# Preparation pipelined by blocks of rows and unrolled; weights of 12 heads combined from raw fp32 in the first chunk's slots; high parts in a slot's first unit

## The chip, the cores and the metric

The kernel runs on one core of a Trainium2 chip. The metric is the device time of one execution in microseconds. TensorE (PE) multiplies, VectorE (DVE), ScalarE (ACT) and GpSimd (POOL) work elementwise, and SyncE (SP) and ScalarE issue the transfers (DMA) between HBM and the on-chip memory.

## The reference

The input is x (2048 rows of 512). It is normalised (xn), and the result is x + attention(xn) + ffn(xn).

```python
q = (x @ wq.T).reshape(B, S, N_HEADS, QK_HEAD)          # 16 heads, 128 + 64
q_nope, q_pe = (q[..., :NOPE], q[..., NOPE:])
q_pe = apply_rope(q_pe, cos, sin)
kv = x @ wkv_a.T                                        # 128 latent + 64 rotary
k_pe = apply_rope(k_pe[:, :, None, :], cos, sin)[:, :, 0, :]
q_lat = jnp.einsum('bshd,hdc->bshc', q_nope, wkv_b_h[:, :NOPE])
kv_cache = rmsnorm(kv_lat, kv_norm_w)
scores = (einsum('bshc,btc->bsht', q_lat, kv_cache) + einsum('bshr,btr->bsht', q_pe, k_pe)) * SCALE
attn = jax.nn.softmax(where(causal, scores, NEG_INF), axis=-1)
out_lat = jnp.einsum('bsht,btc->bshc', attn, kv_cache)
out = jnp.einsum('bshc,hdc->bshd', out_lat, wkv_b_h[:, NOPE:])
attention = out.reshape(B, S, N_HEADS * VDIM) @ wo.T
# ffn: weight rounded to -1, 0, 1 times its mean absolute value, then xn @ w.T + bias
```

## The kernel before

A value of fp32 is held as a sum of two parts of the type fp32r, a high and a low one (names in _h and _l; in Wq, Wp, Wv and xT an index 0 or 1), and a product is made of three: high by high, high by low, low by high. ScalarE mostly writes the high part and VectorE or GpSimd the low one.

Two stages follow each other. `build_prepare` is the preparation. Its loop runs over 4 rounds (the first and last written out, two in a loop on each engine); a round holds one chunk of 512 rows as 4 blocks of 128, and the weights of 4 heads, spread over 16 places s. Places 0 to 3 transpose the normalised blocks (xhat to xT, L774, L550, L647), places 4, 5, 7, 9 make the latent rows and the rotary keys (pKV, L781; GpSimd's powers L471), places 8 to 11 the ffn (pF with ffnT, L800; acc, L655), places 12 to 15 transpose the keys (L812, L814). A head's weights take four places: wo is transposed (L824), the rotary part of wq is put in order by a product with a 0/1 matrix (L833), Wq is the product of wq and wkv_b (pQ, L843) and Wv that of wkv_b and wo (L849). GpSimd writes the low parts of the raw weights (L444, L449, L453). All weights, xT and acc of three chunks go to scratch tensors in HBM. No engine has a queue of its own beside the written order.

`build_attention` is the second stage. It runs over 64 heads of chunks (4 chunks of 16 heads), in slots: a slot of the first chunk is one head and has 4 units; in unit u row block u of the head is scored. In a slot s TensorE makes the scores of head s (p_score, L1124), the latent query of head s+1 (p_lat, units 1 and 2, L1104), in odd slots the rotary queries of two heads (p_rot, unit 0), p_out of head s-2 (units 2 and 3, L1144) and p_result of head s-3 (L1156). The scores are copied to probs (ring of 3, L1196), ScalarE takes exp (L1301), VectorE turns 32x32 squares (L1218), and 16 transfers exchange the quarters (12 by SyncE, L1004, 4 by ScalarE, L1311). Then ScalarE writes the high part of the exchanged probabilities (pT_h, L1322, `high_group`), and GpSimd the low one (pT, L1416). `high_place` says in which slot and unit that stands. A SyncE slot issues the first 8 transfers of an exchange, then the next head's Wv (L1016), which waits for the last p_result product of the head before, then the last 4 of the exchange.

```python
    if k < HIGH_RING:
        return (s + 1, units_of(s + 1) - 1) if phase(s + 1) == 1 else (s + 2, 0 if phase(s + 1) == 3 else 1)
```

## Time and profile before

| what | value |
|---|---|
| median of 3 runs (lowest, highest) | 1833.46 us (1831.61, 1834.55) |
| profiled execution: its time, its span | 1835.66 us, 1833.6 us |
| busy PE, DVE, POOL, ACT | 1715.1, 1210.3, 1008.5, 848.9 us |
| preparation ends, first p_rot product | 175.89 us |
| first score product of slot 0 | 184.8 us |
| DMA in all | 309.12 MB, mean 169 GB/s |

Busy time is the union of an engine's instructions. A matmul's record reaches until its result is out, so neighbours overlap, and the distance of two starts says more of what one costs than its length. PEclk is the granted TensorE clock, 1.00 for 2.4 GHz and 0.50 for 1.2 GHz.

### The profile page before, as it was taken

The numbers are of one execution on the slowest core, as the hardware profiler recorded it, in microseconds if no ns is written. First come the engines' busy times: TensorE is split into PE (matmuls) and PEld (weight loads), VectorE is DVE, ScalarE is ACT, GpSimd is POOL, SyncE is SP. The second block draws the span as 40 slices with busy tenths as digits, with TensorE's granted clock in tenths as the row PEclk, the third lists the DMA queues.
The fourth block names the chain that finished last, engine by engine and source line by source line (L and its number), as shares of the span: only waits on it lengthen the run. The fifth ranks groups of instructions, "written<-read, shape, count | busy, mean of one in ns | idle before, by whom it ended". The sixth has DMA issues, their size and how long they took to land. (4 is left out here: it accounts for less than half of the span.)

```text
span 1833.6 us, 28210 instructions
## 1 busy us (share of the span) xinstructions
PE 1715.1 (94%) x9326; PEld 1448.6 (79%) x9326; DVE 1210.3 (66%) x2801; ACT 848.9 (46%) x1358; POOL 1008.5 (55%) x635
## 2 busy tenths in 40 slices
PE   6998788888999999999999999999999999999996
PEld 5887677666777777778888888888888888888885
DVE  4765465665677667667777767767677666666763
ACT  4554344443444455345544554544544544554442
POOL 4674544443465555455565565565646555565654
PEclk9888899998999999999999999999999999999999
DMA  6995345464766666647555555566756565555553
GB/s 198 372 331 212 105 138 172 134 203 135 196 164 169 173 164 170 195 133 207 151 155 161 144 153 159 158 191 164 191 131 152 146 163 130 158 153 129 148 131 107
DMA packets 127680, 309.12 MB, mean 169 GB/s; under 512 B 29554, under 2 KB 42099, under 8 KB 126388
## 3 DMA queue, kind: packets, MB, share of 16 engines
q1 hardware_dynamic: 98784, 227.04, 44.0%
q10 hardware_dynamic: 28756, 80.35, 16.1%
q8 instruction: 72, 1.18, 0.3%
q14 instruction: 68, 0.56, 0.1%
HBM read 113.28 MB, written 34.60 MB: 81 GB/s over the span
## 5 line engine op out<-in xcount | busy, mean ns | idle before, releaser
L1416 POOL TENSOR_TENSOR pT<-pT,pT_h 128x1024 fp32r<-128x1024 f32 x320 | 688.8, 2181 | 419.8 <-ACT pT_h L1322 418.2
L1196 DVE TENSOR_SCALAR_CACHE_REDUCE probs<-p_score 128x512 f32<-128x512 f32 (+3 forms) x640 | 381.4, 602 | 370.4 <-PE p_score L1124 219.3
L1301 ACT ACTIVATE probs<-probs,neg_max 128x128 f32<-128x128 f32 (+15 forms) x256 | 307.6, 1202 | 438.0 <-DVE neg_max L1202 373.8
L1322 ACT ACTIVATE pT_h<-pT 128x1024 fp32r<-128x1024 f32 x320 | 291.3, 963 | 254.7 <-PE p_out L1144 173.6
L1218 DVE STREAM_TRANSPOSE turned<-probs 128x1024 f32<-128x1024 f32 (+7 forms) x384 | 341.6, 915 | 42.5 <-ACT probs L1301 38.0
L1144 PE MATMUL p_out<-pT_h,V_h 128*128 128x256 f32 (+3 forms) x1024 | 302.7, 296 | 26.6 <-POOL pT L1416 26.5
L1144 PE MATMUL p_out<-pT,V_h 128*128 128x256 f32 (+3 forms) x1024 | 304.2, 297 | 0.0
L1144 PE MATMUL p_out<-pT_h,V_l 128*128 128x256 f32 (+3 forms) x1024 | 303.7, 297 | 0.0
L1124 PE MATMUL p_score<-Kp,qp_h 128*128 128x512 f32 (+3 forms) x640 | 236.3, 369 | 15.3 <-POOL qp_l L1408 15.3
L1124 PE MATMUL p_score<-Kn_h,q_h 128*128 128x512 f32 (+3 forms) x640 | 241.6, 377 | 2.9 <-DVE q_l L1241 2.4
L1144 PEld LDWEIGHTS p_out<-pT_h,V_h 128*128 128x128 f32 x1024 | 196.8, 192 | 51.4 <-issue 34.8
L1124 PE MATMUL p_score<-Kn_l,q_h 128*128 128x512 f32 (+3 forms) x640 | 235.3, 368 | 0.0
L1124 PE MATMUL p_score<-Kn_h,q_l 128*128 128x512 f32 (+3 forms) x640 | 234.0, 366 | 0.0
L1124 PE MATMUL p_score<-Kp,qp_l 128*128 128x512 f32 (+3 forms) x640 | 233.1, 364 | 0.0
L1104 PE MATMUL p_lat<-xT,Wq 128*128 128x512 f32 x768 | 223.5, 407 | 0.0
L1259 DVE SCALAR_TENSOR_TENSOR acc<-p_result,inv_sum,acc 128x512 f32<-128x512 f32 x256 | 189.1, 744 | 42.6 <-PE p_result L1156 38.7
L1144 PEld LDWEIGHTS p_out<-pT_h,V_l 128*128 128x128 f32 x1024 | 197.1, 192 | 14.4
L1156 PE MATMUL p_result<-Wv,o_h 128*128 128x512 f32 x512 | 172.5, 418 | 31.3 <-issue 14.6
L1144 PEld LDWEIGHTS p_out<-pT,V_h 128*128 128x128 f32 x1024 | 197.1, 192 | 4.3
L1104 PEld LDWEIGHTS p_lat<-xT,Wq 128*128 128x128 f32 x768 | 140.6, 193 | 24.5
L1405 POOL TENSOR_TENSOR qp_l<-rotated,qp_h 64x512 fp32r<-64x512 f32 x64 | 82.3, 1286 | 140.7 <-ACT qp_h L1352 133.7
L1124 PEld LDWEIGHTS p_score<-Kp,qp_h 128*128 128x128 f32 x640 | 121.8, 190 | 40.1 <-POOL qp_l L1408 20.9
(135 smaller groups left out, 2352.0 us busy)
## 6 DMA issues: line engine op xcount, KB each, us to landing
pT<-turned SPq DMA_DIRECT2D x384, 128.0 KB, 3.3
Wq<-wq_scr ACTq DMA_DIRECT2D x63, 512.0 KB, 4.7
Wv<-wv_scr SPq DMA_DIRECT2D x63, 512.0 KB, 4.0
pT<-turned SPq DMA_DIRECT2D x192, 112.0 KB, 3.8
pT<-turned SPq DMA_DIRECT2D x192, 96.0 KB, 2.5
pT<-turned ACTq DMA_DIRECT2D x128, 128.0 KB, 3.9
Wp<-wp_scr SPq DMA_DIRECT2D x31, 512.0 KB, 4.7
pT<-turned SPq DMA_DIRECT2D x192, 80.0 KB, 2.8
```

The source lines that it names most:

```text
L1104: mm = pe.matmul(out, weights[:, w, it, :], xT[:, x, it, :], start=(it == 0 and k == 0), stop=(it == IT - 1 and k == 2))
L1124: mm = pe.matmul(out[:, 0:width], q[p][:, rows], kk[:, keys], start=(k == 0), stop=(k == 4 and b < j))
L1144: mm = pe.matmul(out[:, :, cols, :], v[:, t, :], pt[:, :, t - first, rest, :], start=(t == 0 and a == 0), stop=(t == piece_tiles(s) - 1 an ...
L1156: mm = pe.matmul(out[:, :], o[:, rows], Wv[:, w, :], start=(k == 0), stop=(k == 2))
L1196: dve.tensor_scalar(probs[row % ROW_RING][:, b * CW:b * CW + width], p_score[n % SCORE_RING][:, 0:width], SCALE, LOWEST, ALU.mult, ALU.max ...
L1218: last = dve.transpose(to.rearrange("p a t q -> p t a q"), rows.rearrange("p (t a q) -> p t a q", a=4, q=32))
L1259: dve.scalar_tensor_tensor(out=acc[:, i, :], in0=p_result[(QB * g + i) % 2][:, :], scalar=inv_sum[g % 4][:, i:i + 1], in1=acc[:, i, :], op ...
L1301: act.activation(probs[row % ROW_RING][:, 0:width], probs[row % ROW_RING][:, 0:width], ACT.Exp, bias=neg_max[p][:, i:i + 1], scale=1.0, ac ...
L1322: act.activation(high.rearrange("p r t i q -> p r t (i q)"), low.bitcast(F32).rearrange("p r t i q -> p r t (i q)"), ACT.Copy).then_inc(p_ ...
L1405: pool.tensor_tensor(qp_l[p][0:ROPE, :], rotated[own, :], qp_h[p][own, :].bitcast(F32), ALU.subtract).then_inc(qp_ready, 1)
L1416: pool.tensor_tensor(low.rearrange("p r t i q -> p r t (i q)"), low.bitcast(F32).rearrange("p r t i q -> p r t (i q)"), high.bitcast(F32). ...
```

## The change

The preparation's loop is replaced by 20 steps that are written out. Step n handles block n's transposes, block n-1's latent row, block n-2's ffn and block n-3's keys. Buffers that were one chunk wide (x_in, xT, acc, Wp) are there twice, and xhat is normalised by ScalarE with a shift and a scale. The host lays the weights out beforehand: transposed, the rotary rows in order, and per head one tensor `raw` of 128 x 1280 with wq, wo and both halves of wkv_b. Only heads 0 to 3 have Wq and Wv made in the preparation (8 products at steps 1 to 4 and 12 to 15). Those of heads 4 to 15 are made in slots 0 to 11 of the first chunk, in one fp32 product each instead of three of fp32r; raw weights lie in the unused upper columns of probs, staged results in the unused half of pT, and both go to scratch and are read back like before. Last, `high_place` puts the first three high parts of the first chunk's slots (two are there) in unit 0 instead of unit 1.

```diff
-LINEAR_SLOTS = {5: (0,), 6: (1,), 7: (2, 3)}
@@ high_place
-        return (s + 1, units_of(s + 1) - 1) if phase(s + 1) == 1 else (s + 2, 0 if phase(s + 1) == 3 else 1)
+        return (s + 1, units_of(s + 1) - 1) if phase(s + 1) == 1 else (s + 2, 0 if phase(s + 1) in (0, 3) else 1)
+RAW = 2 * D + 2 * RANK
+EARLY = 4
+LATE = H - EARLY
+BLOCKS = NT
+PREP_STEPS = BLOCKS + 4
+WEIGHT_STEPS = {1: 0, 2: 1, 3: 2, 4: 3, 12: 4, 13: 5, 14: 6, 15: 7}
+def raw_of(keep, g):
+    return keep["probs"][g % ROW_RING][:, CW:CW + RAW]
@@ build_prepare, tensor
+            def weights(w):
+                g = w // 2
+                pe.wait_ge(s_raw[g % ROW_RING], 16 * (g // ROW_RING + 1))
+                need(pe, s_w_l, w)
+                if w % 2 == 0:
+                    for it in range(IT):
+                        mm = pe.matmul(pQ[:, it, :], raw_query(keep, g, it), raw_keys(keep, g), start=True, stop=True)
+                else:
+                    mm = pe.matmul(pW[:, :], raw_values(keep, g), raw_output(keep, g), start=True, stop=True)
+                mm.then_inc(s_w, 1)
...
+            for n in range(PREP_STEPS):
+                if n < BLOCKS:
+                    transpose_x(n)
+                if 0 <= n - 1 < BLOCKS:
+                    latent(n - 1)
+                if 0 <= n - 2 < BLOCKS:
+                    linear(n - 2)
+                if 0 <= n - 3 < BLOCKS:
+                    transpose_keys(n - 3)
+                if n in WEIGHT_STEPS:
+                    weights(WEIGHT_STEPS[n])
@@ build_prepare, gpsimd
+            for n in range(PREP_STEPS):
+                if n < BLOCKS:
+                    add_bias(n)
+                if 0 <= n - 2 < BLOCKS:
+                    low_keys(n - 2)
+                if 0 <= n - 1 < BLOCKS:
+                    rotary_key(n - 1)
+                if n % QB == 2 and n // QB + 1 < NCH:
+                    norm(n // QB + 1)
+                if n % 2 and n // 2 < PAIRS:
+                    low_pair(n // 2)
@@ build_attention, sync
+            def load_weights(s):
+
+                sp.wait_ge(wq_made, s + 1)
+                sp.wait_ge(wv_made, s + 1)
+                load_raw(sp, t, keep, stored, s + EARLY + ROW_RING)
...
+                if 1 <= s <= LATE and s - 1 + EARLY + ROW_RING < H:
+                    load_weights(s - 1)
                 if 1 <= s <= SLOTS:
                     exchange(s - 1, (0, 1))
+                if 1 <= s <= LATE:
+                    store_query_weights(s - 1)
@@ build_attention, tensor
+            def make_query_weights(s):
+
+                g = s + EARLY
+                pe.wait_ge(stored["raw"][g % ROW_RING], 16 * (g // ROW_RING + 1))
+                pe.wait_ge(rot_read, (s + 1) // 2 + 1)
+                need(pe, wq_low, s)
+                out = p_rot[:, :].rearrange("p (a c) -> p a c", a=IT)
+                for it in range(IT):
+                    mm = pe.matmul(out[:, it, :], raw_query(keep, g, it), raw_keys(keep, g), start=True, stop=True)
+                mm.then_inc(wq_made, 1)
+
+            def make_value_weights(s):
+
+                g = s + EARLY
+                pe.wait_ge(q_split, s + 2)
+                pe.matmul(p_lat[:, :], raw_values(keep, g), raw_output(keep, g), start=True, stop=True).then_inc(wv_made, 1)
...
+                    if s < LATE and u == made_query_unit(s):
+                        make_query_weights(s)
+                    if s < LATE and u == QB - 1:
+                        make_value_weights(s)
@@ build_attention, scalar
+            def high_value_weights(s):
+                act.wait_ge(wv_made, s + 1)
+                need(act, wv_kept[s % 2], 16 * (s // 2))
+                act.activation(Wv_stage[s % 2][:, 0, :], p_lat[:, :], ACT.Copy).then_inc(wv_high, 1)
```

A piece of ScalarE's order in an even slot in the middle of the first chunk, before. The row ahead is exp of the previous slot's last row; L1311 is its share of the exchange, L1322 the high parts, L1345 the latent query's high part.

```order
L1301 ACTIVATE probs,row_sum<-probs,neg_max 128x512
L1328 ACTIVATE o_h<-p_out 128x4x4x32
L1301 ACTIVATE probs,row_sum<-probs,neg_max 128x128
L1311 DMA pT<-turned 32x512 x4
L1322 ACTIVATE pT_h<-pT 128x1024
L1322 ACTIVATE pT_h<-pT 128x8x64
L1301 ACTIVATE probs,row_sum<-probs,neg_max 128x256
L1301 ACTIVATE probs,row_sum<-probs,neg_max 128x384
L1345 ACTIVATE q_h<-p_lat 128x512
```

The same piece of the changed kernel, where L1262 is exp, L1272 the exchange, L1283 the high parts, L1318 and L1313 the new high parts of Wv and Wq (staged in pT).

```order
L1318 ACTIVATE pT<-p_lat 128x512
L1262 ACTIVATE probs,row_sum<-probs,neg_max 128x512
L1289 ACTIVATE o_h<-p_out 128x4x4x32
L1313 ACTIVATE pT<-p_rot 128x512
L1283 ACTIVATE pT_h<-pT 128x1024
L1283 ACTIVATE pT_h<-pT 128x8x64
L1262 ACTIVATE probs,row_sum<-probs,neg_max 128x128
L1272 DMA pT<-turned 32x512 x4
L1262 ACTIVATE probs,row_sum<-probs,neg_max 128x256
```

The high parts stand ahead of exp of row 0 (128x128) and of the exchange now, and the new high part of Wv ahead of exp of row 3 (128x512).

TensorE at the end of an odd slot of the changed kernel, unit 3: the last p_out products (L1085), then the two new products, then the scores of the next slot (L1065).

```order
L1085 MATMUL p_out<-pT_h,V_h 128x4x32
L1085 MATMUL p_out<-pT_h,V_l 128x4x32
L1085 MATMUL p_out<-pT,V_h 128x4x32
L1034 MATMUL p_rot<-probs 128x128 x4
L1041 MATMUL p_lat<-probs 128x512
L1065 MATMUL p_score<-Kn_h,q_h 128x128
L1065 MATMUL p_score<-Kn_l,q_h 128x128
```

The rows L1034 and L1041 are new; before, the scores followed p_out. In even slots L1034 stands at the end of unit 1.

TensorE in one step of the changed preparation (no weights in it), transposes first.

```order
L714 MATMUL pX<-ident,xhat 128x128 x4
L726 MATMUL pKV<-kvaT_h,xT_even 128x192
L726 MATMUL pKV<-kvaT_l,xT_even 128x192
L726 MATMUL pKV<-kvaT_h,xT_even 128x192 x2
L726 MATMUL pKV<-kvaT_l,xT_even 128x192
L726 MATMUL pKV<-kvaT_h,xT_even 128x192 x2
L726 MATMUL pKV<-kvaT_l,xT_even 128x192
L726 MATMUL pKV<-kvaT_h,xT_even 128x192 x2
L726 MATMUL pKV<-kvaT_l,xT_even 128x192
L726 MATMUL pKV<-kvaT_h,xT_even 128x192
L737 MATMUL pF<-ffnT,xT 128x512 x8
L744 MATMUL pK<-ident,lat 128x128
```

Before, the same kinds stood in four separate quarters of a round, between the weights' products.

## Rows read from the trace of the kernel before

**Rows 1.** The page, its first line.

```profile
span 1833.6 us, 28210 instructions
```

**Rows 2.** Stretches: us, busy us by engine, granted clock, DMA share, GB/s.

```profile
0.00:20.70 20.70, 3.94 (x12) 2.42 (x13) 6.20 (x18) 6.39 (x13) 4.55 (x9) 1.00 0.93 280
...
98.00:136.00 38.00, 35.61 (x216) 31.47 (x216) 25.50 (x58) 20.99 (x58) 26.91 (x39) 0.87 0.96 335
...
267.70:391.10 123.40, 109.73 (x528) 87.32 (x528) 78.73 (x204) 50.09 (x113) 54.48 (x37) 0.94 0.54 154
298.90:302.30 3.40, 3.40 (x9) 2.92 (x10) 1.70 (x3) 1.34 (x3) 2.93 (x3) 0.50 0.48 154
302.30:329.60 27.30, 24.06 (x124) 18.88 (x123) 17.99 (x48) 10.99 (x26) 10.45 (x7) 1.00 0.55 155
```

**Rows 3.** Order of time on PE, third round: start, us, line, out<-in.

```profile
113.77 0.63 PE L833 MATMUL pW<-order,wqp_h 64*128 64x64 f32 x4
...
114.78 0.33 PE L843 MATMUL pW<-wkb_h,wqn_h 128*128 128x128 f32 x1
...
116.17 0.30 PE L781 MATMUL pKV<-kvaT_h,xT 128*128 128x192 f32 x1
...
117.54 0.41 PE L849 MATMUL pW<-woT_h,wkb_h 128*128 128x512 f32 x1
...
118.26 2.02 PE L800 MATMUL pF<-ffnT,xT 128*128 128x512 f32 x8
120.11 0.60 PE L824 MATMUL pW<-ident,wo 128*128 128x128 f32 x4
120.47 0.34 PE L781 MATMUL pKV<-kvaT_h,xT 128*128 128x192 f32 x1
```

**Rows 4.** Groups on POOL in the preparation: count, busy us, mean ns.

```profile
L449 POOL TENSOR_TENSOR wqp_l<-wqp,wqp_h 64x512 fp32r<-64x512 f32 x16 | 22.3, 1395 | 2.3
...
L453 POOL TENSOR_TENSOR wqn_l<-wqn,wqn_h 128x512 fp32r<-128x512 f32 x16 | 20.4, 1277 | 2.6 <-POOL wqp_l L449 0.5
L444 POOL TENSOR_TENSOR wkb_l<-wkb,wkb_h 128x256 fp32r<-128x256 f32 x16 | 12.3, 767 | 25.6 <-ACT wkb_h L521 25.6
```

**Rows 5.** Order of time, the start and the end of the preparation.

```profile
9.26 2.04 PE L855 MATMUL pKV<-rows,ones 1*128 1x512 f32 x2 [9.26 <-DMA mask_f<-in_mask]
...
11.10 0.63 PE L856 MATMUL pKV<-rows,ones 1*128 1x128 f32 x2
...
12.56 2.46 DVE L625 BATCH_NORM_STATS2 stats<-x_in 128x6 f32<-128x512 f32 x4
...
18.96 1.03 POOL L459 TENSOR_TENSOR rstd<-var_eps,minus_half 128x4 f32<-128x4 f32 x1
...
20.72 1.09 PE L774 MATMUL pX<-ident,xhat 128*128 128x128 f32 x4 [7.52 <-DVE xhat L641]
...
26.63 0.42 PE L843 MATMUL pW<-wkb_l,wqn_h 128*128 128x128 f32 x1
...
26.84 0.41 PE L843 MATMUL pW<-wkb_h,wqn_l 128*128 128x128 f32 x1
...
175.89 1.52 PE L1104 MATMUL p_rot<-xT,Wp 128*128 128x512 f32 x3 [2.28 <-PEq L230]
```

**Rows 6.** First chunk: waits in 267.7:391.1 (us, times, longest), then order of time.

```profile
PE p_out L1144 <- POOL pT L1416: 7.2, 8, 1.5
...
PE p_result L1156 <- issue: 4.0, 4, 1.2
...
298.52 0.57 ACT L1345 ACTIVATE q_h<-p_lat 128x512 fp32r<-128x512 f32 x1
298.85 0.75 PE L1144 MATMUL p_out<-pT_h,V_h 128*128 128x512 f32 x1 [1.48 <-POOL pT L1416]
...
309.63 1.58 ACT L1322 ACTIVATE pT_h<-pT 128x1024 fp32r<-128x1024 f32 x2 [3.46 <-DMA pT<-turned]
...
329.46 0.57 ACT L1345 ACTIVATE q_h<-p_lat 128x512 fp32r<-128x512 f32 x1
```

More of the change, by code:

```diff
@@ L775, in transpose_x, with latent @@
                 mm.then_inc(s_xT, 1)
-            def product(out, b, w_h, w_l, done):
-                cols = slice(b * P, (b + 1) * P)
+            def latent(m):
+                cols, x = slice(m % QB * P, (m % QB + 1) * P), xT[m // QB % 2]
+                pe.wait_ge(s_xT_l, m + 1)
+                if m == 0:
+                    pe.wait_ge(s_bcast_out, 2)
+                    pe.wait_ge(s_kva_l, 2)
+                need(pe, s_lat, m - 1)
                 for it in range(IT):
-                    for k, (x, w) in enumerate(((0, w_h), (0, w_l), (1, w_h))):
-                        mm = pe.matmul(out, xT[:, x, it, cols], w[:, it, :], start=(it == 0 and k == 0),
+                    for k, (h, w) in enumerate(((0, kvaT_h), (0, kvaT_l), (1, kvaT_h))):
+                        mm = pe.matmul(pKV[m % 2][:, 0:192], x[:, h, it, cols], w[:, it, :], start=(it == 0 and k == 0),
@@ L798, in linear @@
+            def linear(m):
+                cols, x = slice(m % QB * P, (m % QB + 1) * P), xT[m // QB % 2]
+                if m == 0:
+                    pe.wait_ge(s_tern, 2)
+                need(pe, s_acc, m - 1)
                 for it in range(IT):
-                    for x in range(2):
-                        mm = pe.matmul(pF[b % 2][:, :], xT[:, x, it, cols], ffnT[:, it, :], start=(it == 0 and x == 0),
-                                       stop=(it == IT - 1 and x == 1))
+                    for h in range(2):
+                        mm = pe.matmul(pF[m % 2][:, :], x[:, h, it, cols], ffnT[:, it, :], start=(it == 0 and h == 0),
+                                       stop=(it == IT - 1 and h == 1))
@@ L934, in build_attention @@
         inv_sum = [sb(f"inv_sum{i}", [P, QB]) for i in range(4)]
+        spare = [half[:, :].rearrange("p (a k c) -> p a k c", a=4, k=2)[:, :, 1, :] for half in pT]
+        Wq_stage = [part[:, 0:2, :] for part in spare]
+        Wv_stage = [part[:, 2:4, :] for part in spare]
         p_score = [ps(f"p_score{i}") for i in range(SCORE_RING)]
@@ L1495, in constants, with laid_out @@
         "sinT": by_chunk(np.concatenate([sin, -sin, sin, -sin], 1)),
+    }
+def laid_out(wq, wkv_a, wkv_b, wo, w_ffn):
+    by_input = lambda w: np.ascontiguousarray(w.T.reshape(IT, P, -1).transpose(1, 0, 2))
+    apart = np.concatenate([np.arange(0, ROPE, 2), np.arange(1, ROPE, 2)])
+    heads = wq.reshape(H, QK, D)
+    pairs = heads[:, NOPE + apart, :].reshape(PAIRS, P, D)
+    keys_values = wkv_b.reshape(H, 2, P, RANK).transpose(0, 2, 1, 3).reshape(H, P, 2 * RANK)
+    return {
+        "raw": np.concatenate([heads[:, 0:NOPE, :], wo.T.reshape(H, VDIM, D), keys_values], axis=2),
+        "kvaT": by_input(wkv_a[np.concatenate([np.arange(RANK), RANK + apart])]),
+        "ffnT": by_input(w_ffn),
+        "wpT": np.stack([by_input(w) for w in pairs]),
     }
```

863 lines of the change are left out of this document (386 added, 477 removed).

## The prediction

> **What bounds the kernel now.** I read the busy row first, then the stretches, then the order of time inside two stretches. The profiled span is 1833.6 us [rows 1], its run 1835.66 us, the runs' median 1833.46 us. The change touches the preparation, which ends where the first p_rot product starts at 175.89 us [rows 5], and the first chunk (heads 0 to 15), whose heads 6 to 13 lie in 267.7:391.1 [rows 2]. What follows keeps its instructions and their order; I take its time as it is.
>
> In the preparation, one round (4 blocks of rows and 4 heads' weights) is 38.0 us long, and TensorE is busy 35.61 us of it while GpSimd is busy 26.91 and VectorE 25.50 [rows 2]. Busy overstates TensorE, because matmuls overlap. The starts in [rows 3] say what it needs at the full clock: 1.37 us for a block's 12 pKV products (116.17 to 117.54), 1.85 for its 8 pF products, 0.36 for 4 transposes (120.11 to 120.47), so with half of that again for the keys 1.37 + 1.85 + 0.36 + 0.18 = 3.8 us a block. A head's weights need 1.01 (8 order products), 1.39 (12 pQ products), 0.72 (3 wide ones) and 0.36 (wo transposes), 3.5 us. A round is 4 x (3.8 + 3.5) = 29.2 us, and takes 38.0: a factor of 1.30, made of waits between engines and of a granted clock of 0.87 [rows 2]. DMA is at a share of 0.96 there with 335 GB/s [rows 2], so it is full too, but each round is equally long whatever the traffic, so I hold the chain of TensorE for the bound.
>
> In the first chunk a pair of heads takes 30.94 us (q_h at 298.52 and 329.46 [rows 6]), 15.4 us a head. TensorE's columns per head are: p_lat 12 x 512, p_rot 6 x 512, scores 5 x 1280 and 4 masks of 128, p_out 3 x 1280, p_result 12 x 512, together 26,112. At 512 columns in 0.23 us (pF: 1.85 / 8) that is 11.7 us, with the narrow ones 12.0. So 3.4 us a head is not work. Of it 0.9 is the wait for the low part of pT (7.2 us over 8 heads), 0.5 a wait in front of p_result (4.0 us over 8), which I read as the Wv load, and half of 3.4 us at a granted clock of 0.50 in each pair, 0.85 a head [rows 2, 6]. That half-rate stretch begins right behind the 1.48 us gap at 298.85, and 302.3:329.6 is at 1.00.
>
> **The change, part by part.** (1) The preparation loses 12 heads' weights, and for the 4 left the order products, the wo transposes and the splitting into high and low parts. It becomes 20 steps, in each of which TensorE does one block's transposes, the pKV of the block before, the pF of the one before that, and keys. No round starts with only transposes any more.
>
> Start: the first TensorE transposes stand at 20.72 us, 8.2 us after x_in's statistics started at 12.56 [rows 5]. Now x and ffnT are issued first, 2.1 MB, at the 280 GB/s of the first 20.7 us [rows 2] 7.5 us, so statistics start near 8.3; 2.46 for them, 1.1 for moments, 1.03 for rstd [rows 5] put the first transposes near 14. The first pF products wait for VectorE: two copies, thresholds, comparison, kvaT_l and ternary, some 7 us more. I put step 2's start at 22 us, with TensorE then at half rate: matmuls at 26.63 and 26.84 are 0.21 apart where those at full rate are 1.39 / 12 = 0.12 apart [rows 3, 5].
>
> Steps 2 to 15: TensorE 3.8 us. GpSimd: 26.91 us a round less four times the three low parts it loses (1.395 + 1.277 + 0.767 = 3.44 [rows 4]) is 13.2, 3.3 a block, plus half a pair's low part, 0.64: 3.9 us. The two are level, so I take 4.4 us a step for hand-overs: 14 x 4.4 = 61.6. Seven weight products more: the fp32 ones are bounded by L855 and L856 [rows 5]. The first takes 1.84 us for 512 columns (9.26 to 11.10) at half rate, 0.92 at full; a 128-column one is between a quarter of it, 0.23, and half of L856's 0.63, 0.32. I take 0.28, so pQ's four cost 1.1 and the wide one 0.92: 7.1 us. Last four steps without new rows: 3.6 + 2.2 and the keys' chain, 8 us. Half rate at the start: 5 us. Sum 22 + 61.6 + 7.1 + 8 + 5 = 103.7, taken as 105: 71 us less. Bounds: 92 without any hand-over (22 + 14 x 3.9 + 7 + 8), 109 if steps keep the factor 1.30 ((14 x 3.8 + 7.1) x 1.30 + 22 + 8), 118 with transfers in the way.
>
> Transfers of the preparation: x 4.2, raw 4.6, wpT 2.1, tables and others 3.1, Wq and Wv 4.2, Wp 4.2, xT 6.3, acc 3.1 MB, 31.8 MB; at 335 GB/s 95 us from the first issue at 1 us on. That lies below 105, with little room.
>
> (2) The first 12 slots each gain TensorE 2.0 us (1.1 + 0.92), ScalarE and VectorE two 128x512 evictions each, and 1.7 MB of transfers (raw 0.66, Wq and Wv stores 1.05). Busy VectorE goes from 9.8 (78.73 / 8) to 11.2 us, ScalarE from 6.3 to 7.5, transfers from 154 GB/s [rows 2] to 264, under the 335 of the preparation. Three SyncE issues and their waits stand between exchange issues; those weights are finished in the slot before, so I cost them at nothing; if an exchange lands 1 us later for them, ScalarE's p_high is 1 us later.
>
> The value product is the last of unit 3, and behind it wait, on ScalarE exp of row 3, and on VectorE the last accumulate and row 2's turn (the two orders stand in the section on the change). Today TensorE ends values around 1.4 us after the last scores; product 0.92, ScalarE 0.6, VectorE 0.69 put VectorE back at work some 3.7 us behind the scores (4.8 in odd slots, with the query product). In even slots TensorE then meets p_result before o_l is split, about 1.2 us of new wait every second head; in odd ones the 3 us of p_rot cover it.
>
> (3) High parts move from a slot's unit 1 to unit 0, in front of exp of row 0 and of ScalarE's share of the exchange. At 309.63 ScalarE had waited for the exchange to land [rows 6]; now it waits there with exp of row 0 behind it, so exp of rows 0 to 2 and q_h come 0.5 to 3.3 us later, which lies beside TensorE's work (now TensorE needs the query only at the end of the slot). In return pT's low part is done 1.3 to 3 us earlier, and the 0.9 us wait of TensorE goes.
>
> Sum for a slot with weights: + 2.0 work, - 0.9 pT wait, - 0.5 Wv wait (it lies beside the new products), + 0.6 new wait at p_result: + 1.2; with the half-rate 0.85 back, + 0.35; with the rest of the 3.4 us (1.2 unexplained) partly filled by work, down to - 0.8. I take 0 a head, between - 1.0 and + 2.0. Four heads without weights: - 0.9, and most of the 0.85: - 1.3 each, - 5 us.
>
> What the half clock gives back is my largest choice here. The Trainium skill, "TensorE: Matmul & The Clock Gate", section "HAM oscillation — how this bites in real kernels", says that recurring idle gaps let the engine fall back to half clock every time. By that rule all of 0.85 x 16 = 14 us returns once the gap is closed, by the rows alone (if the stretch stays) none of it; the trace agrees as far as the stretch at 0.50 follows the gap.
>
> Total: 1835.7 - 71 - 5 = 1760 in the profiled execution, 2 less by the median; I say 1760.
>
> **Rivals.** *Forecast*, 0.58: preparation ends at 98 to 112 us, the 12 heads stay at 14.4 to 16.2 us.
> *The first chunk pays in full*, 0.20: VectorE and ScalarE blocked at unit 3 and at the exchange use up every gap, + 2.0 x 12 = 24: 1784. For it: each of the two engines waits in order; against: 3.4 us a head is idle on TensorE.
> *The preparation does not overlap better*, 0.10: engines hand over as before and transfers are full (0.96); end at 118, 58 us less: 1773.
> *Better than forecast*, 0.09: step at 4.1, clock back, 12 heads at 14.4: preparation 98, 12 x -1.0: 1760 - 7 - 12 - 4 = 1737.
> *Slower*, 0.02: exchange landing at unit 0. ScalarE's blocked exp delays its exchange share, which delays the next slot's high parts, so landing joins a loop. It decides from 76 / 12 = 6.3 us a head on; today's longest wait there is 3.46 us.
> *No change*, 0.01: first chunk gives back exactly what the preparation gains, 5 to 6 us a head.
>
> **Numbers.** From 1742 (between better and forecast) to 1786 (first chunk in full): 0.1 below and about 0.1 above. 0.2% is about what a measurement of this kernel tells from no change; the first four cases are all faster: 0.97; same 0.01; slower 0.02.
>
> **What would show it.** First p_rot product near 105 us; GpSimd and TensorE both over 85% busy in 30:90; pT's wait in front of p_out gone and granted clock near 1.00 in the first chunk; q_h to q_h of a pair near 31 us in slots 0 to 11, near 28 in 12 to 15; a VectorE row that waits for the high part of Wv in unit 3. Wrong would be: steps over 5 us in the preparation, waits for x_in or stores, or p_result waiting over 2 us a head.

## The result and the profile after

The changed kernel takes 1765.09 us (median of 4 runs, 1762.51 to 1775.97), beside 1834.01 us (4 runs, 1831.61 to 1838.35) for the kernel before on the same chip: a ratio of 0.9633, with a 95% interval of 0.9589 to 0.9677. The forecast was 1760, in a range from 1742 to 1786. The profiled execution fell by 71.0 us in its span.

The first line of the page after, which answers [rows 1]:

```profile
span 1762.6 us, 27068 instructions
```

The table splits both spans. A stage of the attention goes from the first q_h of one chunk to the first q_h of the next (ScalarE's row on L1345 before, L1308 after), read from the order of time.

| stage, us | before | after | difference |
|---|---|---|---|
| to the first p_rot product (end of the preparation) | 175.9 | 115.5 | -60.4 |
| from there to the first q_h | 7.3 | 5.7 | -1.6 |
| first chunk, heads 0 to 11 | 177.1 | 178.0 | +0.9 |
| first chunk, heads 12 to 15 | 68.9 | 63.1 | -5.8 |
| second chunk | 346.9 | 342.6 | -4.3 |
| third chunk | 450.5 | 451.0 | +0.5 |
| fourth chunk to the end | 607.0 | 606.7 | -0.3 |

The second chunk holds the same instructions before and after, so its -4.3 us are no effect that a single profile can show: over the kernels here that leave that chunk alone it lies between 339.5 and 346.9 us, and a second measurement of the changed kernel gave 345.4. Nor is the -1.6 us ahead of the first q_h an effect: that stretch is 7.2 us in the second measurement. The preparation and the first chunk repeat within 0.5 us; of the first chunk's parts, heads 0 to 11 took 177.0 us there, 0.1 less than before instead of 0.9 more.

**Preparation.** Stretches of the changed kernel, which answer to the round in [rows 2]: us, busy us (instructions) of PE, PEld, DVE, ACT and POOL, granted clock, DMA share, GB/s.

```profile
14.00:30.00 16.00, 13.22 (x65) 11.58 (x65) 13.06 (x26) 7.75 (x18) 8.63 (x12) 1.00 0.69 267
30.00:60.00 30.00, 22.86 (x132) 18.64 (x130) 17.11 (x49) 11.50 (x37) 17.38 (x29) 0.89 0.72 281
60.00:90.00 30.00, 23.22 (x131) 18.51 (x132) 16.36 (x50) 13.89 (x49) 19.01 (x34) 0.94 0.56 204
90.00:115.00 25.00, 21.65 (x133) 17.37 (x131) 13.35 (x37) 12.20 (x43) 15.48 (x33) 1.00 0.94 344
```

The 1.00 of the first row needs care: the trace has no clock record before 25.5 us, and up to 25.3 us the pKV products start 0.21 us apart, behind it 0.11. In 30:90 no column is full: TensorE is busy for 77% of it, GpSimd for 61%, transfers hold 0.72 and 0.56. Something makes all engines wait by turns. The waits of 20:110 name it (engine, tile and line <- releaser: us in total, times, longest):

```profile
DVE Kn_l L643 <- ACT Kp L539: 17.9, 5, 6.5
POOL Wp_even L486 <- ACT Wp_even L545: 17.3, 4, 7.8
ACT Wp_even L545 <- DMA wp_raw<-in_wpT: 17.0, 3, 8.6
...
ACT xhat L512 <- DVE shift L605: 13.6, 3, 5.1
PE pK L744 <- DVE Kn_l L643: 11.7, 6, 5.2
```

The other half of these loads has a row of its own with 5.3 us, 22.3 us together. How one such wait travels is seen in the order of time around 51 us, first the issues of SyncE (SPq), then the engines, with the idle time ahead of each in brackets:

```profile
38.32 0.72 SPq L437 DMA_DIRECT2D xT_scr<-xT_even  x1
39.14 0.98 SPq L386 DMA_DIRECT2D wp_raw<-in_wpT  x1
...
51.20 0.63 ACT L545 ACTIVATE Wp_even<-wp_raw 128x512 fp32r<-128x512 f32 x1 [8.61 <-DMA wp_raw<-in_wpT]
51.74 0.26 ACT L538 ACTIVATE Kn_h<-pK 128x128 fp32r<-128x128 f32 x1
51.89 0.27 ACT L539 ACTIVATE Kp<-pK 128x128 fp32r<-128x128 f32 x1
51.91 1.27 POOL L486 TENSOR_TENSOR Wp_even<-wp_raw,Wp_even 128x512 fp32r<-128x512 f32 x1 [7.76 <-ACT Wp_even L545]
52.05 0.81 ACT L512 ACTIVATE xhat<-x_in,shift,rstd 128x512 f32<-128x512 f32 x1
52.19 0.29 DVE L643 TENSOR_TENSOR Kn_l<-pK,Kn_h 128x128 fp32r<-128x128 f32 x1 [6.50 <-ACT Kp L539]
52.54 0.47 PE L744 MATMUL pK<-ident,lat 128*128 128x128 f32 x1 [5.24 <-DVE Kn_l L643]
```

A pair's rotary weights (256 KB, wp_raw) are asked for at 39.14 and used at 51.20, 12.1 us later. ScalarE stands 8.61 us in front of them. Behind its row wait the keys' high parts, for these VectorE, for VectorE TensorE; and xhat of a later block too. A load that nobody on the critical path needs before the second stage stops the whole pipeline, because each engine takes its rows in the written order.

**First chunk.** Its part 160:300, and TensorE's waits in 121.2:362.3, from the first q_h to that of the second chunk. They answer to the stretch of 123.4 us in [rows 2] and to the waits in [rows 6].

```profile
160.00:300.00 140.00, 134.42 (x697) 107.76 (x697) 100.80 (x252) 66.41 (x147) 61.97 (x41) 1.00 0.82 254
```

```profile
PE p_score L1065 <- POOL qp_l L1386: 7.4, 3, 4.0
...
PE p_result L1097 <- DVE acc L1214: 3.1, 5, 0.6
...
PE p_result L1097 <- DVE o_l L1190: 2.0, 5, 0.4
```

TensorE is busy for 96% of that part, at the full clock. The wait of p_out for the low part of pT is gone; of the kernel before, the same view over its whole first chunk (183.2:429.2) reads:

```profile
PE p_out L1144 <- POOL pT L1416: 12.0, 13, 1.5
PE p_score L1124 <- POOL qp_l L1408: 8.9, 3, 4.0
...
PE p_result L1156 <- issue: 5.2, 6, 1.2
```

The new products, in the order of time of the changed kernel:

```profile
180.15 1.10 PE L1034 MATMUL p_rot<-probs 128*128 128x128 f32 x8
...
181.09 1.02 PE L1041 MATMUL p_lat<-probs 128*128 128x512 f32 x2
...
181.55 0.62 PE L1065 MATMUL p_score<-Kn_h,q_h 128*128 128x128 f32 x1
...
182.15 0.60 ACT L1318 ACTIVATE pT<-p_lat 128x512 fp32r<-128x512 f32 x1 [2.77 <-PE p_lat L1041]
```

From start to start the query products take 0.94 us. The value product is over near 181.95: the scores of the next slot come at their own pace only behind that point, the second of them at 182.01. That is 0.86, 1.80 us a head together. ScalarE's 2.77 us in front of its high part are the wait that the text foresaw in unit 3.

### The profile page after: what moved, and what is told of

Its sections match the earlier page's. It is cut to its first block and busy times, and to the rows that moved or that the text cites. A ratio compares the mean times of both kernels' runs of the same rounds, so it can differ in the third digit from the quotient of the medians.

```text
span 1762.6 us, 27068 instructions
## 1 busy us (share of the span) xinstructions
PE 1662.0 (94%) x9030; PEld 1396.0 (79%) x9030; DVE 1180.8 (67%) x2755; ACT 820.1 (47%) x1295; POOL 963.4 (55%) x595
## 3 DMA queue, kind: packets, MB, share of 16 engines
q1 hardware_dynamic: 89008, 227.04, 44.8%
## 5 line engine op out<-in xcount | busy, mean ns | idle before, releaser
L1262 ACT ACTIVATE probs<-probs,neg_max 128x128 f32<-128x128 f32 (+15 forms) x256 | 307.5, 1201 | 409.2 <-DVE neg_max L1147 334.8
L1283 ACT ACTIVATE pT_h<-pT 128x1024 fp32r<-128x1024 f32 x320 | 291.3, 964 | 232.7 <-PE p_out L1085 177.3
L1085 PE MATMUL p_out<-pT_h,V_h 128*128 128x256 f32 (+3 forms) x1024 | 299.7, 293 | 12.9 <-POOL pT L1394 12.9
L1085 PE MATMUL p_out<-pT,V_h 128*128 128x256 f32 (+3 forms) x1024 | 302.6, 295 | 0.0
L1085 PE MATMUL p_out<-pT_h,V_l 128*128 128x256 f32 (+3 forms) x1024 | 302.1, 295 | 0.0
L1065 PE MATMUL p_score<-Kp,qp_h 128*128 128x512 f32 (+3 forms) x640 | 236.4, 369 | 14.2 <-POOL qp_l L1386 14.0
L1065 PE MATMUL p_score<-Kn_h,q_h 128*128 128x512 f32 (+3 forms) x640 | 242.7, 379 | 2.0 <-DVE q_l L1186 1.7
L1065 PE MATMUL p_score<-Kn_l,q_h 128*128 128x512 f32 (+3 forms) x640 | 234.0, 366 | 0.0
L1065 PE MATMUL p_score<-Kn_h,q_l 128*128 128x512 f32 (+3 forms) x640 | 233.5, 365 | 0.0
L1065 PE MATMUL p_score<-Kp,qp_l 128*128 128x512 f32 (+3 forms) x640 | 232.9, 364 | 0.0
L1085 PEld LDWEIGHTS p_out<-pT_h,V_h 128*128 128x128 f32 x1024 | 196.0, 191 | 32.7 <-issue 17.1
L1085 PEld LDWEIGHTS p_out<-pT_h,V_l 128*128 128x128 f32 x1024 | 196.1, 191 | 14.7
L1085 PEld LDWEIGHTS p_out<-pT,V_h 128*128 128x128 f32 x1024 | 196.0, 191 | 4.0
L1065 PEld LDWEIGHTS p_score<-Kp,qp_h 128*128 128x128 f32 x640 | 121.3, 190 | 40.5 <-POOL qp_l L1386 21.6
```

Source lines behind the costliest of these rows:

```text
L1065: mm = pe.matmul(out[:, 0:width], q[p][:, rows], kk[:, keys], start=(k == 0), stop=(k == 4 and b < j))
L1085: mm = pe.matmul(out[:, :, cols, :], v[:, t, :], pt[:, :, t - first, rest, :], start=(t == 0 and a == 0), stop=(t == piece_tiles(s) - 1 an ...
L1262: act.activation(probs[row % ROW_RING][:, 0:width], probs[row % ROW_RING][:, 0:width], ACT.Exp, bias=neg_max[p][:, i:i + 1], scale=1.0, ac ...
L1283: act.activation(high.rearrange("p r t i q -> p r t (i q)"), low.bitcast(F32).rearrange("p r t i q -> p r t (i q)"), ACT.Copy).then_inc(p_ ...
```

## The experiments

Each edit is made to the changed kernel, but for one that is made to the kernel before. All were measured beside the kernel before on the same chip. "Ratio" is to it. The preparation's end is the first p_rot product, the first chunk is q_h to q_h.

| kernel | median us | ratio (95% interval) | preparation | first chunk | whole span |
|---|---|---|---|---|---|
| e1_pairs_early | 1752.34 | 0.9551 (0.9523 to 0.9578) | 100.6 | 241.2 | 1753.2 |
| e2_norm_late | 1765.63 | 0.9630 (0.9602 to 0.9659) | 114.1 | 239.9 | 1761.5 |
| e4_high_in_unit1 | 1799.08 | 0.9798 (0.9764 to 0.9833) | 114.8 | 273.5 | 1797.9 |
| e6_no_late_weights | 1755.98 | 0.9575 (0.9547 to 0.9602) | 115.6 | 226.9 | 1745.0 |
| e5_before_high_unit0 | 1814.88 | 0.9896 (0.9878 to 0.9913) | 176.9 | 226.9 | 1813.6 |
| e7_late_transfers_only | 1756.71 | 0.9587 (0.9566 to 0.9608) | 115.1 | 230.0 | 1749.8 |
| e8_pairs_and_statistics_early | 1745.66 | 0.9523 (0.9503 to 0.9542) | 95.9 | 241.1 | 1740.7 |
| e9_pairs_early_value_parts_last | 1748.96 | 0.9545 (0.9521 to 0.9568) | 100.5 | 238.8 | 1745.1 |
| a0_changed_again | 1767.08 | 0.9619 (0.9593 to 0.9645) | 115.8 | 240.6 | 1767.9 |
| e10_all_three | 1743.39 | 0.9508 (0.9480 to 0.9535) | 96.5 | 236.9 | 1741.6 |
| e11_store_behind_loads | 1760.35 | 0.9600 (0.9565 to 0.9634) | 111.2 | 240.3 | 1755.8 |

### The preparation

**e1_pairs_early.** SyncE loads each pair's rotary weights one pair earlier; the wait for the buffer keeps its form.

```diff
-                if n % 2 == 0 and 4 <= n and n // 2 < PAIRS:
-                    k = n // 2
+                if n % 2 == 0 and 2 <= n and n // 2 + 1 < PAIRS:
+                    k = n // 2 + 1
```

> The changed kernel with one edit: SyncE issues the load of a rotary pair's raw weights (wp_raw) two steps earlier, ahead of the store of the pair before and of the 2.1 MB xT store, instead of behind them. Theory P (the preparation's steps are long, 6.0 us instead of my 4.4, because ScalarE stands in its order behind a pair load that lands late; 22.3 us of such waits in 20:110, the longest 8.6 us): those waits shrink to below 5 us, the first p_rot product comes at 98 to 104 us instead of 115.45, and the time is 12 to 17 us below the changed kernel's 1765. Rival D (the preparation is full of transfers, the wait only moves to the next transfer): p_rot at 112 us or later, waits for x_in or for the shift grow instead, time within 4 us of 1765. Rival L (each engine's own work, no slack behind the wait): p_rot at 107 to 111.

The preparation ended at 100.6 us, 14.9 earlier, and the whole took 1752.34 us: the theory that the late load held the pipeline stands, its rivals don't. The stretches show the two bystanders come back, TensorE and GpSimd:

```profile
30.00:60.00 30.00, 26.97 (x165) 22.76 (x164) 20.39 (x56) 17.19 (x55) 24.13 (x42) 0.94 0.89 349
60.00:90.00 30.00, 27.83 (x183) 23.92 (x182) 20.60 (x59) 16.83 (x58) 22.72 (x42) 1.00 0.79 303
```

ScalarE waits nowhere for wp_raw in this run. A load took longer from issue to landing (9.1 us in the median, 7.1 in the changed kernel) and cost nothing, since it was asked for in time.

**e11_store_behind_loads.** Is the load late because it is issued late, or because it lies behind the 2.1 MB store of xT that SyncE issues right ahead of it? Here the store stands one step later, and the load where it was.

```diff
-                if n % QB == 3 and n // QB < NCH - 1:
-                    cc = n // QB
+                if n and n % QB == 0 and n // QB <= NCH - 1:
+                    cc = n // QB - 1
                     sp.wait_ge(s_xT_l, QB * (cc + 1))
```

> The changed kernel with one edit: in the preparation SyncE issues the store of a chunk's xT one step later, behind that step's load of a pair's rotary weights, in place of right ahead of it. The load itself is not issued earlier in the program. Theory B (the load is late because it queues behind the 2.1 MB store): the load issued near 39 us lands 5 to 7 us sooner, the longest wait of ScalarE for wp_raw falls from 8.6 us to 4 us or less, and the first p_rot product comes at 104 to 110 us. Rival I (the load is issued too late whatever stands ahead of it, since it waits for the pair two before to be split): the wait keeps 6 us or more, first p_rot product at 113 to 116 us.

The result lies between the two theories. In the order of time, first SyncE's issue and then ScalarE's use:

```profile
38.31 0.74 SPq L386 DMA_DIRECT2D wp_raw<-in_wpT  x1
...
46.74 0.63 ACT L545 ACTIVATE Wp_even<-wp_raw 128x512 fp32r<-128x512 f32 x1 [4.21 <-DMA wp_raw<-in_wpT]
63.04 0.63 ACT L545 ACTIVATE Wp<-wp_raw 128x512 fp32r<-128x512 f32 x1 [6.28 <-DMA wp_raw<-in_wpT]
```

From issue to use it is 8.4 us instead of 12.1, so the store ahead was worth 3.6 us of this load (it was also issued 0.8 us earlier); the Trainium skill, "DMA: Bandwidth & Descriptors", section "Queues, rings and completion order", says that one issuer's descriptors are consumed in the order of its ring, and the trace agrees. But 4.21 us of the wait stayed, and the next pair's load still made ScalarE wait 6.28. The preparation gained 4.3 us of the 14.9 that the earlier issue gives. So the main thing is when the load is issued, a smaller part what lies ahead of it.

**e2_norm_late.** The second row of the waits: ScalarE stands at xhat, 13.6 us, for the shift of the next chunk's statistics. Here xhat of a chunk's first block stands behind the keys' high parts.

```diff
-                if n + 1 < BLOCKS:
+                if n + 1 < BLOCKS and (n + 1) % QB:
                     normalise(n + 1)
...
                 if 0 <= n - 2 < BLOCKS:
                     high_keys(n - 2)
+                if n + 1 < BLOCKS and (n + 1) % QB == 0:
+                    normalise(n + 1)
```

> The changed kernel with one edit: in ScalarE's order the normalising of a chunk's first block, which waits for the shift (13.6 us in three waits, the longest 5.1), stands behind that step's xT, squares and key rows instead of ahead of them. Theory P (the pair load is the main cause and this wait the second): 3 to 8 us less preparation, p_rot at 107 to 112 us. Rival: the transposes of that block now come later and the chain through TensorE takes it back: p_rot at 114 to 118 us.

It ended at 114.1 us, 1.4 earlier: the rival's value. ScalarE's wait at xhat fell from 13.6 to 5.1 us, and most of that came back in other rows of ScalarE: 1.2 us more in front of wp_raw (the longest wait 10.2 us, 8.6 in the changed kernel), and 4.8 us more, 10.0 against 5.2, where it waits for TensorE's latent row, as the rival has it:

```profile
ACT Wp_even L545 <- DMA wp_raw<-in_wpT: 17.2, 3, 10.2
ACT squares L525 <- PE pKV L728: 10.0, 6, 4.1
```

This edit was not made to a kernel whose loads come in time, so what it is worth there is not shown.

**e8_pairs_and_statistics_early.** So the same wait is shortened at its source, on top of the edit of e1: VectorE makes the second half of the next chunk's statistics, and GpSimd its rstd, sooner in their step, ahead of the rotary key. GpSimd's part of the edit:

```diff
@@ gpsimd
                 if 0 <= n - 2 < BLOCKS:
                     low_keys(n - 2)
-                if 0 <= n - 1 < BLOCKS:
-                    rotary_key(n - 1)
                 if n % QB == 2 and n // QB + 1 < NCH:
                     norm(n // QB + 1)
+                if 0 <= n - 1 < BLOCKS:
+                    rotary_key(n - 1)
```

> The changed kernel with the pair loads two steps earlier (as in the first experiment, preparation 100.6 us) and the shift of the next chunk made earlier within its step: VectorE's statistics ahead of the rotary key, GpSimd's rstd ahead of its powers. ScalarE's waits for the shift were 12.2 us in three. Theory W (they are waits on the path now that the pair load is gone): 5 to 9 us less, first p_rot product at 92 to 96 us. Rival (VectorE's statistics now delay the rotary key and the latent row by 2 us in the same steps, and the path runs through them): 99 to 103 us.

It ended at 95.9 us, 4.7 us ahead of e1, at the upper end of what the theory gave. In the whole times the difference is not clear (0.9523 and 0.9551, the intervals overlap). ScalarE's wait for the shift only fell from 12.2 to 9.3 us, so it is not gone; the clock of 30:60, 0.94 in e1 and 1.00 here, gives back some 1.8 us more. Now TensorE is busy for 93% or more from 30 us on:

```profile
30.00:60.00 30.00, 28.90 (x191) 24.97 (x191) 21.07 (x63) 17.93 (x59) 25.22 (x47) 1.00 0.93 357
60.00:90.00 30.00, 27.98 (x177) 23.43 (x177) 19.91 (x60) 17.73 (x61) 23.01 (x41) 1.00 0.90 352
```

The starts of the transposes show what a step costs when nothing is late, 3.83 us from the first to the second row:

```profile
41.78 0.60 PE L716 MATMUL pX<-ident,xhat 128*128 128x128 f32 x4
45.61 0.60 PE L716 MATMUL pX<-ident,xhat 128*128 128x128 f32 x4
49.60 0.66 PE L716 MATMUL pX<-ident,xhat 128*128 128x128 f32 x4
```

In the changed kernel the same steps read:

```profile
43.52 0.60 PE L714 MATMUL pX<-ident,xhat 128*128 128x128 f32 x4
53.02 1.06 PE L714 MATMUL pX<-ident,xhat 128*128 128x128 f32 x4
60.20 0.66 PE L714 MATMUL pX<-ident,xhat 128*128 128x128 f32 x4 [0.21 <-ACT xhat L512]
```

### The first chunk

**e5_before_high_unit0.** One part of the change alone: the kernel before, with the first three high parts of a slot in unit 0.

```diff
-        return (s + 1, units_of(s + 1) - 1) if phase(s + 1) == 1 else (s + 2, 0 if phase(s + 1) == 3 else 1)
+        return (s + 1, units_of(s + 1) - 1) if phase(s + 1) == 1 else (s + 2, 0 if phase(s + 1) in (0, 3) else 1)
```

> The kernel before with one edit: the high parts of the first chunk in a slot's unit 0. The changed kernel without late weights ran its first chunk (first q_h to the 17th) in 226.9 us against 246.0 before, and the changed kernel with the high parts in unit 1 needed 273.5 against 241.1. Theory H (unit 0 is worth about 19 us when a slot has no weights and more when it has): the first chunk takes 225 to 230 us, the preparation stays at 175.9, and the whole is 16 to 21 us below before, a ratio near 0.990. Rival S (part of the 19 us came from the unrolled preparation or from reading the same four heads' weights): 236 us or more.

The first chunk fell from 246.0 to 226.9 us, and the whole by 1.0%, as the theory on the high parts had it. The stretch from q_h to q_h and TensorE's waits in it:

```profile
184.20:411.10 226.90, 197.96 (x982) 162.35 (x982) 144.47 (x386) 94.66 (x214) 110.27 (x71) 0.95 0.56 162
```

```profile
PE p_score L1124 <- POOL qp_l L1408: 17.6, 10, 4.0
...
PE p_result L1156 <- DVE acc L1259: 3.8, 6, 0.6
```

The 12.0 us in front of p_out are gone, and the 5.2 us in front of p_result with them. In their place p_score waits 8.7 us longer for the rotary query's low part:

```profile
298.38 0.33 PE L1124 MATMUL p_score<-Kp,qp_h 128*128 128x128 f32 x1 [1.48 <-POOL qp_l L1408]
```

That is once a pair, 1.48 us long, as p_out's long wait was before ([rows 6], 298.85): the largest wait of a pair has moved from p_out to p_score, and only p_out's small waits (3.1 us) and those of p_result are really gone. GpSimd, which writes this low part, stands idle ahead of it and waits for ScalarE's high part (37.8 us in 15 times). What the clock gives back is worked out from the rows: a mean of 0.92 over 246.0 us (the next fence) is 2 x 0.08 x 246.0 = 39.4 us at the half level, half of which, 19.7, is lost if TensorE has work all the time; 0.95 over 226.9 is 11.3 lost. So -12.0 - 5.2 + 8.7 - 8.4 = -16.9 of the -19.1 us are accounted for. A mean is rounded to 0.01, about 2 us of loss.

The first chunk of the kernel before:

```profile
183.20:429.20 246.00, 208.22 (x982) 166.49 (x983) 144.95 (x386) 95.07 (x215) 110.00 (x71) 0.92 0.52 149
```

**e4_high_in_unit1.** The reverse: the changed kernel with that line put back.

```diff
-        return (s + 1, units_of(s + 1) - 1) if phase(s + 1) == 1 else (s + 2, 0 if phase(s + 1) in (0, 3) else 1)
+        return (s + 1, units_of(s + 1) - 1) if phase(s + 1) == 1 else (s + 2, 0 if phase(s + 1) == 3 else 1)
```

> The changed kernel with the high parts of the first chunk back in a slot's unit 1. Nothing else differs. Theory H (my prediction's step 3: unit 0 takes away TensorE's wait for pT's low part, 0.9 us a head, and with the gap the half-rate stretch of the clock, up to 0.85 us a head): the first chunk from the first q_h to the 17th takes 14 to 28 us longer than the 241 us of the changed kernel, pT waits in front of p_out return to 6 us or more over eight heads, granted clock falls towards 0.94. Rival O (ScalarE standing at the exchange costs in unit 0 what the wait cost in unit 1, or the new products fill the gap anyway): within 5 us.

The first chunk grew by 32.4 us, more than the theory's upper end of 28. Its stretch and its first wait:

```profile
120.50:394.00 273.50, 228.62 (x1102) 179.62 (x1101) 160.84 (x408) 106.64 (x237) 109.91 (x71) 0.93 0.66 204
```

```profile
PE p_out L1085 <- POOL pT L1394: 21.2, 13, 2.9
```

The wait for pT is back and nearly twice as long as in the kernel before. The likely reason is that ScalarE, held 44.8 us in front of the new value parts, and VectorE behind it come later to what the high parts of pT in unit 1 need; no run separates that. With the clock (0.93 over 273.5 loses 19.1 us, 0.96 over 241.1 loses 9.6, on the same terms) that makes 21.2 + 9.5 = 30.7 of the 32.4 us. The move is worth 19.1 us without the new weights and 32.4 with them; the two parts of the change don't simply add.

**e6_no_late_weights.** The changed kernel without the making of the weights of heads 4 to 15: no products, no splitting, no raw loads and stores in the slots. Those heads read the weights of heads 0 to 3 again.

```diff
-                    if s < LATE and u == made_query_unit(s):
-                        make_query_weights(s)
-                    if s < LATE and u == QB - 1:
-                        make_value_weights(s)
```

> The changed kernel without the weights of heads 4 to 15 in the first chunk: no raw load, no product, no eviction and no store of them; heads read the stored weights of heads 0 to 3 again instead, so the output is another one. The preparation is unchanged. Theory F (my prediction: products lie mostly in idle time of TensorE, at about 1.0 to 1.3 us a head net): first chunk 10 to 18 us shorter than the changed kernel's 241 us, a pair of heads near 28.3 us in all slots. Rival G (they cost TensorE's 2.0 us in full): 24 us or more shorter. Rival N (free): under 5 us.

The first chunk is 226.9 us, 14.2 less: the middle theory. It is also the value of e5, where the same chunk runs without this work. 1.8 us of products in 12 slots are 21.6 us of TensorE alone, so at least 7.4 of them fill idle time, in front of p_score above all: this kernel waits 18.1 us there, the changed one 7.4.

```profile
PE p_score L1057 <- POOL qp_l L1365: 18.1, 9, 4.0
```

**e7_late_transfers_only.** As e6, but the raw loads are made and stores of the same size leave, from a buffer that is at hand; so it leaves out the products and the splitting, and those heads' weights are not made.

```diff
-                sp.dma_start(t["wv_scr"][s + EARLY], Wv_stage[s % 2].bitcast(F32)).then_inc(wv_kept[s % 2], 16)
+                sp.dma_start(t["wv_scr"][s + EARLY].rearrange("p w c -> p (w c)"), Kn_l[:, 2 * D:4 * D].bitcast(F32)).then_inc(wv_kept[s % 2], 16)
```

> The changed kernel with only the transfers of the late weights: raw loads and stores of the same sizes at the same places of SyncE's order (the stores read Kn_l instead of the staged results, their waits are on the query's low part), but no products and no evictions, so the output is another one. Without anything late the first chunk took 226.9 us, with everything 241.1. Theory E (engines: product time, and ScalarE and VectorE held at unit 3, make the 14.2 us): 227 to 231 us. Rival T (transfers: exchange landings stretch from 254 GB/s of traffic and from SyncE's longer order): 236 us or more.

230.0 us: of the 14.2 us the transfers cost 3.1, products and splitting 11.1. Traffic in the chunk was 240 GB/s, against 162 in e6. The clock alone can make those 3.1 us: 0.93 over 230.0 us loses 16.1, the 0.95 of e6 over 226.9 loses 11.3. Whether the traffic brought it down isn't shown.

```profile
121.00:351.00 230.00, 201.16 (x983) 163.92 (x984) 144.61 (x386) 94.79 (x216) 110.33 (x71) 0.93 0.77 240
```

**e9_pairs_early_value_parts_last.** On top of e1, the high and low parts of Wv stand behind the last exp and the last turn of their unit, so that neither engine is held ahead of that work.

```diff
@@ scalar
                 if s < SLOTS:
                     exp_row(g, first_row(s) + rows_of(s) - 1)
+                if s < LATE:
+                    high_value_weights(s)
```

> The changed kernel with the pair loads two steps earlier, and in the first chunk the high and low part of the value weights behind exp of row 3 (ScalarE) and behind the accumulate and the turn of unit 3 (VectorE) instead of ahead of them. My prediction said that both engines are held there (ScalarE's wait for the product 23.9 us and VectorE's for the high part 17.1 in 160:300). Theory E (that order costs part of the 1.2 us a head): first chunk 232 to 237 us instead of 241.1, the whole at 1743 to 1748. Rival P (TensorE's own 1.7 us of products are the cost, the held engines catch up): 239 us or more, the whole near 1752.

The first chunk became 238.8 us, 2.4 less than in e1 and outside of what the theory of held engines gave and 0.2 under the bound of its rival, by which the products' own time is what they cost; the rival is nearer. The waits that it aimed at shrank all the same, ScalarE's from 28.2 us to

```profile
ACT pT L1318 <- PE p_lat L1041: 5.1, 9, 0.6
```

and VectorE's from 20.6 to 10.8. But the two engines did not come free: ScalarE's wait in front of exp for neg_max grew from 55.9 us in e1 to 71.4, that at the exchange from 30.8 to 40.1, and VectorE's for the scores from 31.3 to 41.8. So 33 us of waiting of two engines beside the bound one mostly moved to other rows, and were worth 2.4 us. In the whole the difference to e1 (0.9545 against 0.9551) can't be told from none.

**a0_changed_again and e10_all_three.** The changed kernel once more, and the edits of e8 and e9 together.

> The changed kernel once more, with no edit, beside the two versions below on one chip, to say how far a repeat lies from the first measurement. Both theories: 1760 to 1770 us; the first p_rot product at 115 to 116 us; the first chunk (first latent query to that of head 16) 240 to 242 us.

> The changed kernel with three edits together: pairs' rotary weights loaded one pair earlier, statistics ahead of the latent row and rotary key, and the high and low part of a head's new value weights behind the last exp and the last turn of their unit. Theory S (the gains add, since the first two lie in the preparation and the third in the first chunk): first p_rot product at 95 to 97 us, first chunk 238 to 240 us, whole 1741 to 1745 us, 2 to 4 us under the version with the first two alone. Rival R (transfers of the first chunk are now the limit, so that a start 20 us earlier is given back in it): first chunk 242 us or more and the whole not under 1745 us.

The repeat stands at 0.9619, inside the interval of the first measurement. All three edits together give 1743.39 us, 5% under the kernel before: preparation 96.5, first chunk 236.9 (3.7 under the repeat, a little more than the theory gave). What the preparation gained is not given back. Whether it beats e8 alone the whole times don't resolve (0.9508 and 0.9523, intervals overlapping).

## Why the prediction came out as it did

**Preparation: -71 us predicted, -60.4 measured; the step that failed.** The step was "so I take 4.4 us a step for hand-overs: 14 x 4.4 = 61.6". With the weights (7.1) and the half rate (5) it made 5.26 us a step. Measured, the transposes of step 2 start at 23.4 and those of step 15 at 101.8: 6.03 a step, 10.0 us over in 13 steps. The rest of the sum held: step 2 at 22, measured 23.4; from step 15 on 13.3 us, measured 13.65. So 1.4 + 10.0 + 0.35 make the 11.75 us between 103.7 and 115.45. What stood in the place of hand-overs was one late load and one late chain of statistics: with both edits of e8 the same 13 steps take 4.62 us each, weights included, and TensorE's price of a step, 3.8 us, is met to 0.03 where nothing is late. So TensorE's price was right, the allowance for hand-overs and half rate was even too large for a pipeline without late inputs, and what was missing is a term for inputs that aren't there. The 5 us for half rate were put at the start, where only some 2 us of step 2 ran at it; the 0.89 and 0.94 of 30:90 lose 5.1 us by the same working as above, beside the late inputs, and in e8 they are gone. The text read the transfers as a sum of bytes (31.8 MB, "below 105, with little room") and never followed SyncE's order step by step. That would have shown the 256 KB of wp_raw behind 2.1 MB of xT, with ScalarE's keys behind their use. The test that the text set itself, "steps over 5 us in the preparation", fired.

**The 12 heads with new work: 0 predicted, +0.9 measured (-0.1 in the repeat).** The products cost 1.80 us a head instead of 2.0. The new wait in front of p_result, put at 1.2 us every second head, was 0.4 (2.0 us in 5 times). The engines held in unit 3 showed as foreseen (12 waits of VectorE, 12 of ScalarE) and cost little: e9 gains 2.4 us without them. The net was nearly exact, and its parts were too large on both sides: the new work alone, counted without the gain at pT, was put at 2.1 us a head (2.0 - 0.5 + 0.6), 25 us in all, and e6 gives 14.2 (12.1 of them in these heads); the gain from the high parts is 12.5 us in e5's first 12 heads, where 0.9 + 0.85 a head make 21. The reading of the 0.5 us in front of p_result as the load of Wv holds. In the kernel before, all six of these waits end 0.09 us behind a landing of Wv, here that of 308.21:

```profile
303.88 0.33 SPq L1016 DMA_DIRECT2D Wv<-wv_scr  x1
308.30 0.70 PE L1156 MATMUL p_result<-Wv,o_h 128*128 128x512 f32 x2 [1.01 <-issue]
```

New products do cover it: in e4, which has them and the high parts in unit 1, 0.7 of the 5.2 us are left. But so does the move of the high parts alone, in e5, where Wv lands before TensorE comes to it. So either part of the change brings these 0.5 us, and the sum rightly has them once.

**Heads 12 to 15: -5 predicted, -5.8 measured.** Here the gain of the high parts stands alone, and e5 shows -6.6 for the same four heads.

**The clock.** The text held 0.85 x 16 = 14 us for what would return if the rule were the whole story, and put most of it into its sum. The granted clock of the first chunk went from 0.92 to 0.96:

```profile
121.20:362.30 241.10, 218.67 (x1102) 176.12 (x1103) 159.23 (x410) 107.46 (x239) 110.11 (x71) 0.96 0.74 229
```

That is 19.7 us lost before and 9.6 after, 10 us back, and between 160 and 300 us it is at 1.00. The five half-rate stretches of 3.4 us that came back once a pair from 268 us on, 8.5 us lost, are all gone; they are what the 0.85 us a head were read from. What loss is left lies at the start of the chunk (before 160) and at its end (behind 330). By the rule of the Trainium skill that the prediction names ("TensorE: Matmul & The Clock Gate", "HAM oscillation — how this bites in real kernels") all of the 14 us would return; 10 did. But that each fall of the clock comes from the one gap of 1.48 us ahead of it isn't shown, and two runs speak against it. In e5 a gap of this length stands in each pair, at p_score, and behind the first of them the clock falls (242.8 us), but five more follow at full clock. In e4 the clock is full for 85 us, in which TensorE is busy for only 85% and waits for pT four times, up to 2.0 us; the next fall stands behind a fifth wait, of 2.6 us. First e5, then e4:

```profile
246.20:396.40 150.20, 135.98 (x708) 111.74 (x706) 105.68 (x275) 66.80 (x152) 73.97 (x49) 1.00 0.62 185
183.40:268.70 85.30, 72.54 (x378) 57.00 (x378) 54.06 (x135) 36.57 (x81) 31.00 (x21) 1.00 0.76 239
```

The page's own case has longer waits than these. So the clock came back when TensorE's waits were closed, as the prediction chose, but what brings it down in the kernel before stays open.

**What follows: unchanged, as taken.** Third and fourth chunk agree within 0.5 us. The second chunk's -4.3 us and the -1.6 ahead of the first q_h fell in the forecast's favour by chance, so that the miss in the whole is only 5 us where the terms of the preparation missed by 10.

**The rivals.** The preparation's 115.5 us lie outside of the forecast's 98 to 112 and near the 118 of the rival in which engines hand over as before. That rival had also held transfers to be full, and they weren't: 0.72 and 0.56 in 30:90. They are nearly full in e8 (0.93 and 0.90), whose preparation ends 20 us sooner, so traffic was not what set the end. The first chunk in full (+24) is contradicted by +0.9. The loop through the exchange, the slower rival, never closed.

## What to carry to other kernels

Follow the issuing queue through a new pipeline step by step, as is done for the engines: a small load that is issued one step before its use, behind a large store, stops every engine whose written order runs past that use, and a sum of bytes doesn't show it. Where no engine and no queue is full in a stretch, read the waits for the one that ends at a DMA, and move its issue before anything else is moved. And a wait on the engine that bounds a stage is worth closing before work is added there: the same one line was worth 19 us without the added work and 32 with it, while 33 us of waits of the engines beside it, which mostly came back in other rows, were worth 2.4. Look where a wait goes that an edit closes: in e5 the longest wait of a pair only moved from p_out to p_score.

## What was unexpected of the hardware

- A load's time from issue to landing says little alone. The 256 KB loads took 5.5 to 12.0 us in the changed kernel and 6.9 to 12.1 in e1, with no wait for them there; one of them took 12.0 us behind a store of 2.1 MB and 8.4 without it.
- Transfers at a share of 0.90 to 0.93 (352 to 357 GB/s) stood beside a TensorE that was busy for 28 to 29 of 30 us, and its steps kept their price of 3.8 us.
- One plain fp32 product stands in for three of fp32r, and is dearer or cheaper by its width: at the full clock four of 128 columns took 0.94 us where the twelve of pQ took 1.39, and one of 512 columns some 0.86 where the three wide ones took 0.72 [rows 3].
- One and the same gap of TensorE, 1.48 us once a pair of heads, stood beside a fall of the granted clock in every pair from 268 us on in the kernel before, and beside full clock for five pairs in e5.
- The stage of 16 heads with 1555 matmuls varied from 339.5 to 346.9 us between kernels that don't differ in it (336.3 in e6, which reads other weights there), and by 2.8 between two profiles of the same kernel, while the first chunk of that same kernel repeated within 0.5. It goes with TensorE's idle time (15.8 to 22.5 us) and with the granted clock (0.98 to 1.00); what sets these was not looked into.
